# Projection stage: the middle tap of both gate tiles, made by ScalarE and added by GpSimd, instead of that of one

## The reference, cut to what matters

```python
z = rmsnorm(u, pre_norm_w) @ in_proj_w.T                 # 512 x 768 for each of 16 batches
zc = z.transpose(0, 2, 1)
z_pre = conv_general_dilated(zc, short_w, ..., padding=[(K - 1, 0)], feature_group_count=3 * D)   # K = 3 taps
z_pre = z_pre + short_b[None, :, None]
x2, x1, v = jnp.split(z_pre, 3, axis=1)
xv = x1 * v                                              # goes into the long convolution
y = (yconv + xv * D_skip[None, :, None]) * x2            # x2 is the gate
```

## Time and profile before

| | |
|---|---|
| median of 3 runs | 2202.64 us (2199.43 to 2203.69) |
| the profiled execution, its own time | 2202.95 us |
| its span in the trace | 2201.2 us |
| mean granted TensorE clock | 0.963 |
| the projection in the trace | from the start to about 213 us |

### The profile page before, as it was taken

One profiled execution on the slowest core, in us unless ns is written; L12 is line 12 of the kernel. 1 busy time (PEld: TensorE's weight loads), 2 busy tenths in 40 slices (PEclk: granted clock), 3 DMA queues, 4 the chain that ended last, 5 costly groups with the idle time before them and its releaser, 6 DMA issues. The chain is left out here.

```text
span 2201.2 us, 39395 instructions
## 1 busy us (share of the span) xinstructions
PE 1984.8 (90%) x12896; PEld 1348.3 (61%) x12960; DVE 1468.1 (67%) x2652; ACT 1221.5 (55%) x2425; POOL 881.2 (40%) x1336
## 2 busy tenths in 40 slices
PE   6886959999999858999999999999999999968997
PEld 4665337888888744566556666566665665535554
DVE  6898634555555427778778777777777777724776
ACT  6775535555555423655656656665656656545554
POOL 3443615555555421343334433334333433232222
PEclk9999969999999969999999999999999999988999
DMA  3343121222111253333444344343443344111221
GB/s 116 120 152 121 48 77 67 77 76 72 69 68 68 76 106 87 80 93 78 103 102 94 71 100 103 79 106 72 103 106 83 83 88 94 43 39 62 82 87 66
DMA packets 104786, 188.10 MB, mean 85 GB/s; under 512 B 27960, under 2 KB 78136, under 8 KB 98488
## 3 DMA queue, kind: packets, MB, share of 16 engines
q1 hardware_dynamic: 104632, 186.13, 31.6%
HBM read 110.23 MB, written 58.79 MB: 77 GB/s over the span
## 5 line engine op out<-in xcount | busy, mean ns | idle before, releaser
L1731 DVE TENSOR_REDUCE at_mneg<-at_ps_s 128x1 f32<-128x384 f32 (+3 forms) x704 | 437.7, 636 | 108.2 <-PE at_ps_s L1369 89.5
L1504 ACT ACTIVATE at_pt<-at_ps_w 128x512 f32<-128x512 f32 x640 | 377.4, 597 | 235.6 <-PE at_ps_w L1380 235.5
L1594 POOL TENSOR_SCALAR_AFFINE_SELECT at_pt<-at_pt 128x256 f32<-128x256 f32 (+1 forms) x640 | 232.3, 365 | 577.9 <-ACT at_pt L1504 575.3
L1368 PE MATMUL at_ps_s<-at_ks,at_qs 96*128 96x128 bf16 (+3 forms) x1024 | 259.9, 307 | 36.0 <-DVE at_mneg L1731 21.6
L1380 PE MATMUL at_ps_w<-at_qs,at_ks 97*128 97x512 bf16 (+3 forms) x1024 | 244.6, 301 | 9.1 <-ACT at_pt L1504 5.1
L1368 PEld LDWEIGHTS at_ps_s<-at_ks,at_qs 96*128 96x128 bf16 x1024 | 85.9, 99 | 226.8 <-DVE at_mneg L1731 140.0
L895 POOL TENSOR_TENSOR ml_m_lo<-ml_m,ml_m_hi 128x512 fp32r<-128x512 f32 x80 | 115.7, 1447 | 179.6 <-ACT ml_m_hi L801 179.4
L1396 PE MATMUL at_ps_o<-at_pt,at_val 128*32 128x512 f32 (+3 forms) x2048 | 168.5, 448 | 9.7 <-POOL at_pt L1594 9.6
L1369 PE MATMUL at_ps_s<-at_mask,at_ident 128*128 128x128 bf16 (+1 forms) x640 | 148.7, 232 | 0.0
L834 ACT ACTIVATE ml_gl<-ml_ps_g 128x512 f32<-128x512 f32 x96 | 56.6, 589 | 152.2 <-PE ml_ps_u L127 148.4
L1380 PEld LDWEIGHTS at_ps_w<-at_qs,at_ks 97*128 97x128 bf16 x1024 | 88.4, 98 | 62.5 <-ACT at_pt L1504 15.4
(11 more groups left out here) (255 smaller groups left out, 5580.6 us busy)
## 6 DMA issues: line engine op xcount, KB each, us to landing
parts_d<-at_parts SPq DMA_DIRECT2D x64, 384.0 KB, 2.5
at_ks<-parts_d SPq DMA_DIRECT2D x192, 128.0 KB, 7.9
at_qs<-parts_d SPq DMA_DIRECT2D x32, 384.0 KB, 5.6
pj_xin<-in_x SPq DMA_DIRECT2D x16, 512.0 KB, 5.3
gate_d<-pj_zc SPq DMA_DIRECT2D x16, 512.0 KB, 2.7
xv_all<-pj_turned_xv SPq DMA_DIRECT2D x16, 512.0 KB, 4.2
ml_turned_y<-xv_all SPq DMA_DIRECT2D x16, 512.0 KB, 3.4
ml_x<-gate_d SPq DMA_DIRECT2D x16, 512.0 KB, 4.3
```

The lines of the kernel that those rows point to most:

```text
L1368: pe.matmul(out[:, i, :], qs[par][0:ROWS, h, toks], ks[par][0:ROWS, h, 0:(qt + 1) * P], start=i == 0, stop=False)
L1504: act.activation(pt[u % RING][:], ps_w[u % 2][:], ACT.Exp, scale=SCALE).then_inc(exped, 1)
L1594: pool.affine_select(out=diag, in_=diag, compare_op=ALU.is_ge, fill=0.0, base=0, pattern=pattern, channel_multiplier=-1).then_inc(cut, 1)
L1731: dve.tensor_reduce(mneg[:, g, h0 % HG:h0 % HG + count, qt], view_score(ps_s[s % 2], qt, count), AX_X, ALU.max, negate=True).then_inc(maxe ...
```

## The change

Both gate tiles, k = 4 and k = 5, are now side tiles. ScalarE makes tap 1 of both, each into a buffer of its own (`side[0]` for k = 4, `side[1]` for k = 5; before, the two buffers were for even and odd batches), GpSimd adds both behind its two products, and VectorE does their two tap 0 last in the batch. ScalarE may write a side buffer when the addition of the batch before has read it. VectorE no longer does tap 1 for k = 5, and its block transposes stand directly behind `low`.

```diff
--- before.py
+++ after.py
@@ -233,8 +233,8 @@
 
     CT = 3 * KT
     ORDER = [2, 4, 3, 5, 0, 1]
-    SIDE = 4
-    DONE = [1, 2, 3, 4, 6, 5]
+    SIDES = (4, 5)
+    DONE = [1, 2, 3, 4, 5, 6]
     with ExitStack() as ctx:
         n = Names(nc, ctx, "pj")
         ident = n.sb("ident", [P, P])
@@ -380,9 +380,10 @@
                         wait(act, gated, KT * (b - 1))
                     act.activation(zc[par][:, ct, :], ps_z[ct][:], ACT.Identity, bias=tb[:, ct:ct + 1],
                                    scale=tap[:, ct, 2:3]).then_inc(tap2_done, 1)
-                    if k == SIDE:
-                        wait(act, side_added, b - 1)
-                        act.activation(side[par][:], ps_z[ct][:], ACT.Copy, scale=tap[:, ct, 1:2]).then_inc(side_set, 1)
+                    if k in SIDES:
+                        n_side = SIDES.index(k)
+                        wait(act, side_added, 2 * (b - 1) + n_side + 1)
+                        act.activation(side[n_side][:], ps_z[ct][:], ACT.Copy, scale=tap[:, ct, 1:2]).then_inc(side_set, 1)
                     if k == 1 and not last:
                         norm(b + 1, 1 - par)
                     if k == 3 and not last:
@@ -433,9 +434,10 @@
                     wait(pool, chunked, KT * (b - 1) + k + 1)
                     pool.tensor_tensor(xv[par][:, k, :], zc[par][:, KT + k, :], zc[par][:, 2 * KT + k, :],
                                        ALU.mult).then_inc(gated, 1)
-                pool.wait_ge(side_set, b + 1)
-                ct = ORDER[SIDE]
-                pool.tensor_tensor(zc[par][:, ct, 1:T], zc[par][:, ct, 1:T], side[par][:, 0:T - 1], ALU.add).then_inc(side_added, 1)
+                for n_side, k in enumerate(SIDES):
+                    pool.wait_ge(side_set, 2 * b + n_side + 1)
+                    ct = ORDER[k]
+                    pool.tensor_tensor(zc[par][:, ct, 1:T], zc[par][:, ct, 1:T], side[n_side][:, 0:T - 1], ALU.add).then_inc(side_added, 1)
                 if isinstance(b, int) and b < 4:
                     prepare_filters(b)
             over_late(pool, B, step)
@@ -507,7 +509,7 @@
                     dve.scalar_tensor_tensor(zc[par][:, ct, 2:T], ps_z[ct][:, 0:T - 2], tap[:, ct, 0:1],
                                              zc[par][:, ct, 2:T], ALU.mult, ALU.add).then_inc(tap0_done, 1)
 
-                direct = [k for k in range(CT) if k != SIDE]
+                direct = [k for k in range(CT) if k not in SIDES]
                 for n, k in enumerate(direct):
                     ct = ORDER[k]
                     dve.wait_ge(tap2_done, CT * b + k + 1)
@@ -519,8 +521,9 @@
                         low(b + 1, 1 - par)
                 chunk(0)
                 chunk(1)
-                dve.wait_ge(side_added, b + 1)
-                tap0(ORDER[SIDE])
+                for n_side, k in enumerate(SIDES):
+                    dve.wait_ge(side_added, 2 * b + n_side + 1)
+                    tap0(ORDER[k])
                 if isinstance(b, int) and b == 3:
                     sum_filters()
             over_late(dve, B, step)
```

## The result

The changed kernel takes 2212.55 us (median of 6 runs, 2210.75 to 2216.30) and the kernel before, in 6 runs, 2202.55 (2199.43 to 2206.25). The ratio is 1.0052, with an interval of 1.0032 to 1.0072: 10 us or half a per cent slower. The forecast was 2213.4, slower. The profiled execution took 2212.83, with a span of 2210.9.

A forecast was written before the change was run, and what follows sets the result against it. The prediction took a loop of dependences over `norm`, 11.68 us a batch, as the bound, not VectorE. Its terms, 3.9 + 5.0 + 0.2 + 1.6 = 10.7 on 2202.95, less 0.3 for the median, gave 2213.4 us, range 2205 to 2220.

The forecast's parts named there:

- the loop over the norm: Dependences from tap 0 of k = 3 over `norm`, transposes and matmuls to the next tap 0: sets the 11.68 us period.
- GpSimd's loop: Beside the first loop, over second product, addition and the root's two parts to `norm`: 0.61 us of slack.
- (a): VectorE loses tap 1 of k = 5, about 0.78 us each: costed at nothing for the loop, only lengthening a wait.
- (b): ScalarE's one more side tap a batch, 0.57 us: the squares end 0.57 later, `norm` is not moved by ScalarE.
- (c): GpSimd's second addition in the loop, 1.26 us: uses up the slack, delays `norm` by 0.39 in ten steps, +3.9 us.
- (d): First four steps, with filter work between addition and root: the whole addition of 1.26 us lands each time, +5.0 us.
- (e): Last batch: VectorE's gain turns into a wait for the second addition, +0.2 us.
- (f): First batches, TensorE idle longer before the transposes: one more fall of the clock to 1.2 GHz, +1.6 us.
- Rival 1: VectorE is the bound after all and the lost tap gains 11 us, 2192 us; chance 0.06.
- rival 2: GpSimd's second addition stays hidden and the loop keeps its period, about 2203 to 2206 us; chance 0.10.
- rival 3: The clock falls in the loop too, in one step of three, and in all four first steps, 2220 us; chance 0.15.
- rival 4: GpSimd's second addition takes its lower bound of 1.04 us, 2210 us; counted within the forecast's own chance of 0.69.

The follow-up runs named there:

- kernel 3: The kernel before with VectorE's tap 1 of k = 5 left out and nothing in its place: 2198.31 us, ratio 0.9969.
- 9: The kernel before with GpSimd's filter work ahead of the products and ScalarE's norm ahead of tap 2 of k = 1: 2189.53 us, ratio 0.9941.
- kernel 10: The kernel before with only ScalarE's norm of the next batch moved ahead of tap 2 of k = 1: 2194.77 us, ratio 0.9963.
- kernel 1: The changed kernel without GpSimd's second addition, ScalarE still making both side taps: 2199.97 us, ratio 0.9986.
- kernel 8: The changed kernel with 13 idle matmuls on TensorE ahead of the transposes in batches 1 to 3: 2209.21 us, ratio 1.0039.
- kernel 2: The kernel before with a second GpSimd addition behind the real one, on data nobody uses: 2211.38 us, ratio 1.0037.
- kernel 4: The changed kernel with GpSimd's root between the two additions and VectorE's tap 0 of k = 5 put off into the next batch: 2213.64 us, ratio 1.0043.

## Why the prediction was right

**The bound before** was right: the loop over the norm held the kernel before at 11.65, and the next one stands at 11.09, where the prediction has 11.07. Kernels 3, 9 and 10 show it. What the prediction calls GpSimd's loop are two, though, as it counts the root's wait of 0.35 into it: one over the squares, which is the 11.07, and one over product and addition. Behind the addition the root could have started at 117.80 + 1.30 + 0.09 = 119.19 and not at 119.45, so that loop was 0.26 shorter, 10.81; 1.26 more makes it the 12.07 of the forecast.

**(a)** VectorE's tap costs nothing in the loop: shown by kernel 3. The wait before k = 3 was to grow to about 1.5. It grew to 1.16, and a new one of 0.24 stands before k = 2 (the row at 120.32), together 1.40.

**(b)** The squares end later and hide: shown by kernel 1, 0.58 for the forecast 0.57.

**(c)** 10 x 0.39 = 3.9; measured 3.78. The second addition takes 1.24 to 1.26 more of GpSimd's time (2.54 and 2.56 for two, 1.30 for one). The estimate worked out from the figure of the Trainium skill, GPSIMD Engine Reference, section Performance versus the Vector engine, was 1.12, which would make the loop 11.93 and the term 2.5; the trace says 12.04, so the measured instruction was the one to take. The page has GpSimd take about twice VectorE's time for the same two-input instruction; no run here has the same instruction on both engines, and 1.30 against VectorE's 0.75 for a tap is 1.7 times.

**(d)** 4 x 1.26 = 5.0; measured 4.99 with the clock held up (kernel 8), 1.25 and 1.24 in the two steps that need no correction.

**(e)** +0.2 for the tail. Measured +0.14 between the tap 0 of k = 3 in batch 14 (197.21 before, 207.94 after, +10.73) and the last tap 0 (+10.87 on the earlier trace rows). VectorE waits in the last batch for the product (0.42) and for the additions (0.18 and 0.47):

```profile
220.49 1.04 DVE L506 STREAM_TRANSPOSE pj_turned_xv<-pj_xv 128x512 f32<-128x512 f32 x1 [0.42 <-POOL pj_xv L435]
221.72 0.75 DVE L509 SCALAR_TENSOR_TENSOR pj_zc<-pj_ps_z,pj_tap,pj_zc 128x510 f32<-128x510 f32 x1 [0.18 <-POOL pj_zc L440]
222.94 0.75 DVE L509 SCALAR_TENSOR_TENSOR pj_zc<-pj_ps_z,pj_tap,pj_zc 128x510 f32<-128x510 f32 x1 [0.47 <-POOL pj_zc L440]
```

**(f)** The mechanism was right, the count was not: two falls more, where I took one, but two of the four are cheaper. 5.14 for the four less two at 1.59 is 2.0, the term was 1.6. The cheaper ones come late: at 36.27 and 67.06 the eight transposes still take 1.09 or 1.10, where 1.73 to 1.97 goes with a fall ahead of them, and only the matmuls of k = 3 behind them are slow. There ScalarE waits 2.90 for k = 3 (the first row) in place of the 3.51 of the earlier trace rows:

```profile
39.78 0.78 ACT L381 ACTIVATE pj_zc<-pj_ps_z,pj_tb,pj_tap 128x512 f32<-128x512 f32 x1 [2.90 <-PE pj_ps_z L127]
...
55.20 0.78 ACT L381 ACTIVATE pj_zc<-pj_ps_z,pj_tb,pj_tap 128x512 f32<-128x512 f32 x1 [3.54 <-PE pj_ps_z L127]
```

The Trainium skill, TensorE: Matmul & The Clock Gate, Part 1, has the clock fall when TensorE goes idle; kernel 8 agrees in three of its gaps, where work took the falls away, while the fourth, idle for 3.29 us (last section), had no fall either.

The sum on the stage was 10.7 and the trace has 10.9; the runs have 10.0. Rival 1 (VectorE bound) falls with kernel 3, rival 2 (hidden) with kernel 2, rival 3 (the clock falls in the loop) with the ten steps, nine at 11.99 to 12.08 and the last at 11.92, and rival 4 (an addition of 1.04) with the 1.24 to 1.26 of (c). Part of the hit is luck. The small errors of (c) and (f) have opposite signs. More than that, the price of the falls isn't fixed: in kernel 2, which has the same addition and as many falls, the four steps take 7.8 us more than the 56.14 of kernel 8, against 5.1 in the changed kernel; falls like those would have made it 2.6 us slower. Single runs of one kernel lie 5 to 7 us apart.

## What to carry to other kernels

Follow the loop of dependences from one batch to the same instruction of the next and write down the slack of the loop beside it. Here one tap 2 moved out of the first loop gave 5.7 us in ten batches (kernel 10) and 1.26 us added to the second cost 3.8, while 0.78 us taken from the busiest engine gave nothing in the loop (kernel 3). Work given to an engine that is idle 60% of the time is free only in the gap where it waits: ahead of a late release, not between that release and the instruction that others wait for. And a reordering moves every queue behind it, SyncE's list of transfers too (kernel 4).

## What the runs showed of the hardware

**The time of a run goes with its mean granted clock.** Over 87 runs of the kernel before, on four chips, the median was 2204.5 us for the 14 runs with a mean clock of 0.960 to 0.962, 2203.8 for the 23 at 0.964 and 2195.9 for the 7 at 0.970; fitted by a line, 1.2 us for each 0.001. On the same program and the same chip that is a spread of 10 us, as much as this change is worth. Kernel 3 shows how it confuses: its six runs at 0.963 to 0.965 took 2199.2 to 2203.2, the three at 0.969 some 2192. Why some runs are granted more I can't say, and as the falls are part of the mean, this shows what goes together and not which is the cause.

**The length of an idle gap does not tell whether the clock falls.** In the kernel before it fell behind gaps of 2.02 and 2.04 us ahead of the transposes and stayed up behind 2.19 and 2.63; in kernel 8 it stayed up behind one of 3.29, the fourth, which had no idle matmuls, while in the loop of kernel 4 it fell once behind 1.87 and stayed up behind 2.04. The row of kernel 8:

```profile
77.76 1.09 PE L454 MATMUL pj_ps_t<-pj_ident,pj_xn 128*128 128x128 f32 x8 [3.29 <-ACT pj_xn L345]
```
